# Filling half of the attention stacks from GpSimd's queue in place of the sync engine's

## What is computed

```python
x = x + attention(layernorm(x), Wqkv, Wout, bout)
x = x + ffn(layernorm(x), Ws1, Ws2, W1, W2, Wr)

# attention, per batch and head
num = exp(q_rot @ k_rot.T / 4)                 # q, k after the rotation by position
den = sum(exp(q @ k.T / 4), axis=-1)           # q, k as projected
attn = where(causal, num / den, 0.0)
y = attn @ v                                   # then y @ Wout + bout

# ffn: a shared expert, squared relu between Ws1 and Ws2, plus routed experts
prob = trunc(softmax of the two best router logits)   # is 0 unless one weight is 1
```

## Time and profile before

| | us |
|---|---|
| median of 3 runs | 1792.62 (1785.33 to 1794.18) |
| the profiled execution | 1789.91 |
| its span | 1788.3 |
| ACT busy in it | 1604.2 (90%) |
| PE busy in it | 1540.1 (86%) |
| VectorE busy in it | 825.0 (46%) |
| POOL busy in it | 511.7 (29%) |

### The profile page before, as it was taken

One profiled execution on the slowest core, in us unless ns is written; L12 is line 12 of the kernel. 1 busy time (PEld: TensorE's weight loads), 2 busy tenths in 40 slices (PEclk: granted clock), 3 DMA queues, 4 the chain that ended last, 5 costly groups with the idle time before them and its releaser, 6 DMA issues.

```text
span 1788.3 us, 29579 instructions
## 1 busy us (share of the span) xinstructions
PE 1540.1 (86%) x8371; PEld 611.4 (34%) x8416; DVE 825.0 (46%) x1818; ACT 1604.2 (90%) x2639; POOL 511.7 (29%) x868
## 2 busy tenths in 40 slices
PE   2888988898988998889988988988888898989885
PEld 1322333333423333233332333433343333423334
DVE  4333424565236543365433753347433565336315
ACT  1899999998999978999899998999989998999990
POOL 3223223322133231232323322223123422233210
PEclk7999999999999989999999999999999999999996
DMA  5233233331333322333223324233133431333200
GB/s 167 75 120 95 80 98 107 113 121 42 102 106 124 104 71 78 106 121 98 93 79 114 109 81 131 77 115 107 60 116 106 127 110 51 98 107 106 89 25 24
DMA packets 95039, 172.44 MB, mean 96 GB/s; under 512 B 15504, under 2 KB 82064, under 8 KB 82576
## 3 DMA queue, kind: packets, MB, share of 16 engines
q1 hardware_dynamic: 94272, 169.15, 29.9%
q10 hardware_dynamic: 592, 1.18, 0.2%
HBM read 111.55 MB, written 58.72 MB: 95 GB/s over the span
## 4 chain that ended last, share of the span: by engine, by line
issue 38%; ACT 21%; PE 21%; POOL 11%; DVE 5%; DMA 1%; SPq 1%; DVEq 1%; POOLq 0%; ACTq 0%
ACT scores L486 14%; ACT probs L496 6%; PE scores L542 5%; POOL parts L402 5%; PE scores L549 4%; PE y_ps L571 4%; POOL rot L400 3%; POOL probs L392 2%; POOL x_acc L431 1%; PE side L581 1%; PE side L601 1%; PE side L622 1%; SPq L315 1%; ACT probs L498 1%; PE side L608 1%
## 5 line engine op out<-in xcount | busy, mean ns | idle before, releaser
L486 ACT ACTIVATE scores<-scores 128x1024 f32<-128x1024 f32 x1024 | 1045.1, 1026 | 21.0 <-PE scores L542 20.5
L542 PE MATMUL scores<-stack 96*128 96x512 bf16 x2048 | 589.2, 386 | 68.3 <-ACT scores L486 36.4
L496 ACT ACTIVATE probs<-scores 128x1024 f32<-128x1024 f32 x512 | 492.3, 1025 | 102.3 <-PE scores L549 99.8
L549 PE MATMUL scores<-stack 96*128 96x512 bf16 (+3 forms) x1536 | 336.9, 335 | 64.8 <-ACT scores L486 26.9
L392 POOL TENSOR_SCALAR_AFFINE_SELECT probs<-probs 128x256 f32<-128x256 f32 (+1 forms) x640 | 228.6, 383 | 409.9 <-ACT probs L496 247.7
L571 PE MATMUL y_ps<-probs,v_sb 128*32 128x512 f32 (+3 forms) x3072 | 332.9, 506 | 4.8 <-ACT probs L496 4.8
L542 PEld LDWEIGHTS scores<-stack 96*128 96x128 bf16 x2048 | 161.9, 98 | 442.3 <-ACT scores L486 224.2
L402 POOL TENSOR_TENSOR parts<-rest,parts 128x512 bf16<-128x512 f32 x124 | 143.3, 1156 | 342.0 <-DVE parts L866 342.0
L549 PEld LDWEIGHTS scores<-stack 96*128 96x128 bf16 x1536 | 124.7, 99 | 334.7 <-ACT scores L486 154.0
L400 POOL TENSOR_TENSOR rot<-raw,cos_sb 128x512 f32<-128x512 f32 x62 | 87.3, 1408 | 445.0 <-DVEq L876 445.0
L486 ACT ACTIVATION_READ_ACCUMULATOR scores<-scores 128x1 f32 x1024 | 204.2, 199 | 0.0
(11 more groups left out here) (126 smaller groups left out, 1129.2 us busy)
## 6 DMA issues: line engine op xcount, KB each, us to landing
stack<-qk_parts SPq DMA_DIRECT2D x762, 128.0 KB, 2.6
qk_parts<-parts SPq DMA_DIRECT2D x127, 384.0 KB, 2.6
out<-x_mid SPq DMA_DIRECT2D x32, 256.0 KB, 2.4
x_in<-in_L_attn_x SPq DMA_DIRECT2D x7, 1024.0 KB, 5.5
x_in<-in_L_attn_x SPq DMA_DIRECT2D x2, 512.0 KB, 4.0
stack<-qk_parts ACTq DMA_DIRECT2D x6, 128.0 KB, 4.8
probs<-in_L_attn_Wqkv SPq DMA_DIRECT2D x1, 512.0 KB, 6.2
cos_sb<-in_cos SPq DMA_DIRECT2D x1, 512.0 KB, 6.9
```

The lines of the kernel that those rows point to most:

```text
L486: nc.scalar.activation(src, src, ACT.Exp, scale=SCALE, accum_out=den[:, g % 2, i, j:j + 1]).then_inc(exp_done, 1)
L496: nc.scalar.activation(probs[:, chunk % 2, j, :], src, ACT.Exp, scale=SCALE).then_inc(exp_done, 1)
L542: mm = nc.tensor.matmul(tile[:, half * HALF:(half + 1) * HALF], q[:, j, i * P:(i + 1) * P], k[:, j, half * HALF:(half + 1) * HALF], start= ...
L549: mm = nc.tensor.matmul(tile[:, col:col + n], k[:, h, i * P:(i + 1) * P], q[:, h, q0:q0 + n], start=True, stop=True)
```

## The change

The twelve DMAs of the rotated stack are issued by POOL. SP issues those of the plain stack as before, and still sends all parts. In POOL's program the fill stands at the step that is `LOW_LAG` + `FILL_LAG` = 7 behind the tile `("qk", 3)`: steps 33, 25, 26 and 31 of groups 0 to 3. POOL waits on `rot_sent` first. For the very first group the rotated fill stands behind POOL's four first low parts.

```diff
+FILL_LAG = 4
...
                                 sp.sem_inc(held["sp"], 1)
-                            fill_stacks(b, g, kind, sent, stacked)
+                            if kind == 0:
+                                fill_stacks(b, g, kind, sent, stacked)
...
             first_parts(1, 1, rot_sent)
-            fill_stacks(0, 0, 1, rot_sent, rot_stacked)
             batch(0, True, False)
...
+            def fill_rotated(b, g):
+                parity = g % 2
+                pool.wait_ge(rot_sent, at(b, 8 * 16, 2 * 16 * (g + 1)))
+                pool.sem_inc(held["pool"], 1)
+                src = scratch[1].rearrange("c s (d h) t -> c s d (h t)", h=HG)
+                for a, terms in enumerate((Q_TERMS, K_TERMS)):
+                    for term, part in enumerate(terms):
+                        pool.dma_start(stack[term:ROWS:TERMS, parity, 1, a, :], src[part, a]).then_inc(rot_stacked[parity], 16)
...
                         kind, t = SIDE[g].get(s - LOW_LAG, ("none", 0))
+                        b1, g1 = (b, g + 1) if g < G - 1 else (b + 1, 0)
                         if kind == "qk" and runs("qk", g, first, last):
-                            b1, g1 = (b, g + 1) if g < G - 1 else (b + 1, 0)
                             low_part(b1, g1, t)
+                        if s - LOW_LAG - FILL_LAG in SIDE[g] and SIDE[g][s - LOW_LAG - FILL_LAG] == ("qk", 3) and \
+                                runs("qk", g, first, last):
+                            fill_rotated(b1, g1)
...
                                         ).then_inc(low_ready, 1)
+            fill_rotated(0, 0)
             pool.wait_ge(more_loaded, 16 * MORE_LOADS)
```

## The result

The changed kernel takes 2063.49 us in the median of 4 runs (2057.04 to 2073.85), the kernel before 1793.4 us in the same session. The ratio is 1.151, with a 95% interval of 1.144 to 1.158: 15% slower. The forecast was 2238 us with a range of 2040 to 2400. The direction and the place were right; the size was too large by 175 us.

The account below looks back on a forecast made before the run. ACT's exponentials were taken to bound the kernel, PE close behind. Lateness 3.4, POOL's DMAs 372, restart 68 and start 4.6 sum to 448 us, added to 1789.9: 2238 us, range 2040 to 2400.

Parts of the forecast that it names:

- What bounds it: Whole kernel: ACT's exponentials set the pace at 90% busy, PE follows at 86%; fills in the loop cost only 4.8 us.
- SP's next work: SP's queue: twelve issues a fill (7.45 us) removed, next work 10 us or more later, so worth 0.
- The wait holds the masks: POOL's queue: masks of chunk 3 (chunk 2 in group 1) stand behind the `rot_sent` wait; PE waits, then ACT.
- release minus product sums: PE's masked product: lateness is release + 12 d + 2.94 − start, giving 3.9, 2.8, −2.5, 1.0 plus 12 d for groups 0 to 3.
- The size of d: POOL's queue: time one DMA issue holds POOL, put at 1.0 us between SP's 0.62 and POOL's 1.41.
- 372 d: POOL's twelve DMAs in each of 31 fills, at 1.0 us each: 372 us.
- Rival 1: POOL issues as fast as SP or faster, 0.3 to 0.75 us each: about 1935 to 2092 us; chance 0.22.
- The restart: PE starts slow after each stall, costing ACT 2.2 us beyond PE's idle, times 31: 68 us.
- cushion: ACT's slack before a late PE product makes it idle: 1.2 us, taken for every group.
- The start: Kernel's first rotated fill: twelve issues by POOL instead of SP make PE start 4.6 us later.
- rival 2: POOL's issue is dearer, over 1.2 us, because POOL shares a port with VectorE: 2396 us at 1.41; chance 0.20.
- The signs: Profile after: twelve DMAs of about 1 us, then masks; PE idle about 10 us 31 times; ACT idle 440 us more, share 72%.

Follow-up runs that it names:

- the wait alone: Against the changed kernel, POOL waits on `rot_sent` at the same place but issues no DMA, SP issues all fills; 1870.96 us, ratio 1.046 to the kernel before.
- The extra products: Changed kernel plus unused PE products ahead of the held product in groups 0, 1 and 3 (21 of 31 stalls); 2035.61 us, against 2066.52 without.
- half of the fill: Against the changed kernel, POOL waits and issues only the six q-side DMAs, SP the six k-side ones; 1966.63 us, ratio 1.098 to the kernel before.
- the fill in the gaps: Changed kernel with the send ahead of the plain fill and POOL's fill at steps 37, 27, 27, 37; 1802.39 us, ratio 1.0025 to the kernel before.

## Why the prediction was right or wrong

- **What bounds it, and nothing to win from SP:** right. ACT runs the same instructions, and 266 of the 275.6 us are its idle time.
- **SP's next work:** it was said to come 10 us or more after the fill. In group 3 it does not: four stores of the output stand right behind it (at 1109.87 in the kernel before). In the changed kernel they run beside POOL's fill and take 5.54 to 6.29 us in place of 2.52. Nothing waits for them, so the term stays 0.
- **The wait holds the masks:** right. The release minus product sums gave PE's idle time with d = 0 as 3.9 and 2.8 us for groups 0 and 1; with the wait alone PE stood 3.56 and 2.82 us. With the measured d (0.487, so 5.8 us for twelve) they give 9.8, 8.7, 3.3 and 6.8 us for groups 0 to 3 of the changed kernel, 222 us in all. The trace has 10.0, 9.4, 2.2 and 6.6 in the mean, 219.6 in all. That it comes so close is in part luck, since two errors cancel: POOL's first DMA comes 3.45 us after the start of the send in the median, where SP's came 3.01 after it, and the eight masks then take 2.48 us in place of 2.94.
- **The size of d:** this is the step that failed. I took 1.0 us, between SP's issue and POOL's slowest product. The trace has 0.487 in the median, 0.492 in the mean, under SP's own 0.589. The term 372 d is 183 us in place of 372, which is 189 us of the error. The estimate from the Trainium skill ("DMA: Bandwidth & Descriptors", the table at the head), about 1 us from the time to the first byte, was no better: that is a latency. The trace has 2.9 us from issue to landing against SP's 2.6, yet POOL was held for less time than SP. Rival 1, with d from 0.3 to 0.75, had 0.22; its sum with 0.487 would have been 3.4 + 181 + 68 − 2 = 250 us.
- **The restart:** 2.2 us a stall was set. ACT's idle time in its three groups of exponentials grew by 263.5 us (154.3 + 80.9 + 28.3) and PE waited 219.6 us for masks: ACT lost 44 us more, 1.4 a stall, on top of the cushion that was used up, so 2.6 by the sum's own way of counting, 81 us in place of 68. The extra products won back some 1.5 us a stall. How the 2.6 divides between cushion, slow clock and PE's backlog of work is not shown: the 1.2 us of cushion were read in one group and taken for all.
- **The rest:** 250 us against 275.6 in the profiled runs. Some 13 us are the restart, 9.3 are ACT's busy time, which the sum took as unchanged, and 3 are idle time of ACT before its other instructions. Why ACT's busy time grew is not shown.
- **The start:** 4.6 us later was forecast. No such loss can be seen: the twelve issues took 5.94 us in place of 7.45, and PE began 8.7 us after the first of them, where it was 9.5:

```profile
42.60 5.94 POOL L413 DMA_DIRECT2D stack<-qk_parts  x12 [7.08 <-DMA qk_parts<-parts]
51.30 1.01 PE L563 MATMUL scores<-stack 96*128 96x512 bf16 x2 [21.35 <-DMA stack<-qk_parts]
```

  Since POOL's first DMA also came half a microsecond later behind the send, the gain is about 0.3 us.
- **VectorE's port (rival 2):** not seen in these DMAs. The twelve take 5.81 us in all four groups alike, but for the holes of the last section. In the changed kernel VectorE has little work meanwhile (0 to 2.0 us), but with the fill behind the masks of chunk 3 it has more. The stretch of the twelve DMAs of group 1 shown in that section (VectorE is the third):

```profile
1023.83:1029.64 5.81, 5.46 (x43) 2.08 (x42) 4.21 (x15) 5.81 (x13) 5.81 (x13) 1.00 0.74 203
```

  VectorE works for 4.21 of the 5.81 us, and the issues take no longer.
- **The signs:** POOL's DMAs came twelve in a row with the masks right behind them, PE waited for masks 31 times, and SP's waits for `rot_sent` are gone, all as said. The sizes were off with d: 0.49 us each, PE's waits 7.1 us in the mean (2.2 in group 2, under the 5 us that were to mean a small d), ACT's idle time up by 266 us and not 440, its share 78% and not 72. The slow clock was expected in each stalled stretch; in group 2 five of eight products behind the stall took 0.64 us.
- **The range:** 2063 us lies near its lower end, which was put there for SP's price of an issue. So the range held because it took in rival 1, not because of the forecast's own d. It also helped that the restart and ACT's busy time, both too low in the sum, go against the error in d.

## What to carry to other kernels

When work is put into an engine's queue, the price is not the work but what it makes late: twelve DMAs of the same size on POOL cost nothing, 16 us or 188 us according to their place and to the wait ahead of them (the last from the ratios of the changed kernel and of the wait alone). Look for the gap in the queue that is long enough, on every path through the loop, and check what releases the wait that comes with the work; here a send that stood behind another queue's fill was half of the loss. PE also came back at half its clock from stalls of 3.6 us, and at times of 1.4, so short stalls can cost more than their length.

## What the runs showed of the hardware

- An issue of 16 rows of 8 KB holds POOL for 0.487 us (384 of them, 0.487 to 0.672), less than SP's queue (0.589 in the median), and lands 0.3 us later (2.9 against 2.6 us).
- POOL's row of DMAs has a hole of 2.31 us at three places of the changed kernel, two in group 1 and one in group 3. The first two:

```profile
636.90 3.90 POOL L413 DMA_DIRECT2D stack<-qk_parts  x8 [8.35 <-DMA qk_parts<-parts]
643.11 1.92 POOL L413 DMA_DIRECT2D stack<-qk_parts  x4 [2.31 <-issue]
...
1268.70 3.90 POOL L413 DMA_DIRECT2D stack<-qk_parts  x8 [8.33 <-DMA qk_parts<-parts]
1274.91 1.92 POOL L413 DMA_DIRECT2D stack<-qk_parts  x4 [2.31 <-issue]
```

  Counted from the start, the holes come behind POOL's 128th, 248th and 368th DMA. That holds in all eight runs in which POOL issues 372 or 384, whatever stands around them, and with half of the fill, where POOL issues 192, the only hole is behind the 128th. The holes there last 1.9 to 2.8 us. So they go by the number of DMAs, from the 128th on one every 120, and not by what SP does: no store runs beside the first, and five other fills run beside stores without a hole. What happens in them is not shown.
- Eight masks back to back took 2.48 us behind a stall and 2.94 in the kernel before, with VectorE at work. With the fill behind the masks of chunk 3, VectorE is held as well: an instruction on 8 columns, 0.17 us in the median, starts 1.1 us before the end of POOL's twelve DMAs of group 1 and ends 0.4 us behind the addition into `x_acc` that follows them (1029.65 to 1034.17). It was so in five of the eight batches.

```profile
1028.52 6.04 DVE L821 TENSOR_SCALAR root<-root 128x8 int32<-128x8 int32 x1
```

  Both fit a port that the two engines share; which instructions hold it was not tested.
- The Trainium skill ("SBUF — State Buffer", the DMA trap of VectorE and SWDGE) warns that VectorE's copies hold up descriptors written by GpSimd. The fills of the changed kernel do not put it to the test, since VectorE makes no copy in those stretches (in the one shown above it is 0.00 us busy from 1075 to 1085). With the plain fills on POOL, VectorE's copies `rest<-rden` and `rot<-rden` fall into the twelve issues of groups 1 and 2, which then take 5.89 to 5.96 us in place of 5.78, 0.2 us more at most; with the fill in the gaps they fall into those of group 2, and five of seven took 5.78 or 5.79 all the same. Whether these copies are of the kind that the page means, no run here shows.
